# An adaLN transformer block on one core: four VectorE operations and one GpSimd group put elsewhere in the hand-written order

## The reference

```python
h = layernorm(x) * (1 + ca) + sa
Q, K, V = h @ Wq.T + bq, h @ Wk.T + bk, h @ Wv.T + bv      # 16 heads of 16
Q, K = elu(Q) + 1, elu(K) + 1
KV = einsum('bshd,bshe->bhde', K, V);  K_sum = K.sum(axis=1)
Z = 1 / (einsum('bshd,bhd->bsh', Q, K_sum) + 1e-6)
x = x + ga * (einsum('bshd,bhde,bsh->bshe', Q, KV, Z) @ Wo.T + bo)
h = layernorm(x) * (1 + cb) + sb
logits = cosine(h, centroids) + h @ w_route.T              # 8 experts
gates = softmax over the two largest logits, else 0
x = x + gb * sum_e gates_e * (gelu(h @ w1_e + b1_e) @ w2_e + b2_e)
```

## Time and profile before

| what | value |
|---|---|
| median of 3 runs | 365.79 us (365.43 to 366.67) |
| profiled execution, its own time | 366.65 us |
| its span | 364.6 us |
| TensorE busy | 349.9 us (96%) |
| VectorE, GpSimd, ScalarE busy | 286.7, 260.5, 234.0 us |
| granted TensorE clock | 1.00 |

### The profile page before, as it was taken

One profiled execution on the slowest core, in us unless ns is written; L12 is line 12 of the kernel. 1 busy time (PEld: TensorE's weight loads), 2 busy tenths in 40 slices (PEclk: granted clock), 3 DMA queues, 4 the chain that ended last, 5 costly groups with the idle time before them and its releaser, 6 DMA issues.

```text
span 364.6 us, 8796 instructions
## 1 busy us (share of the span) xinstructions
PE 349.9 (96%) x2780; PEld 327.3 (90%) x2780; DVE 286.7 (79%) x820; ACT 234.0 (64%) x516; POOL 260.5 (71%) x358
## 2 busy tenths in 40 slices
PE   7999999998999996899999999999999999999995
PEld 7877888887888996899998999999999999999895
DVE  4769767567776989989999898898898988886754
ACT  4376787888978764648557485584674855855541
POOL 4346899877977667787897878889889877655210
PEclk9999999999999999999999999999999999999999
DMA  7941640000000032142240322422314314324211
GB/s 267 331 155 34 202 144 0 2 1 2 0 2 3 1 119 89 40 135 89 61 144 21 127 90 60 135 79 78 104 54 131 87 58 145 89 59 146 93 54 58
DMA packets 23713, 31.79 MB, mean 87 GB/s; under 512 B 2288, under 2 KB 14204, under 8 KB 23680
## 3 DMA queue, kind: packets, MB, share of 16 engines
q1 hardware_dynamic: 23240, 31.34, 27.6%
q10 hardware_dynamic: 440, 0.04, 0.1%
HBM read 27.04 MB, written 4.34 MB: 86 GB/s over the span
## 4 chain that ended last, share of the span: by engine, by line
PE 75%; DVE 16%; issue 4%; DMA 2%; ACT 2%; DVEq 0%; ACTq 0%
PE bank L795 21%; PE bank L796 19%; PE bank L797 19%; PE bank L803 4%; PE bank L850 3%; DVE hid_g L1348 2%; PE bank L827 2%; DMA g_bc<-in_b 2%; DVE bank L1365 2%; PE bank L978 2%; DVE early L1265 1%; PE bank L903 1%; DVE gT_f L1404 1%; PE bank L1020 1%; DVE den L1296 1%
## 5 line engine op out<-in xcount | busy, mean ns | idle before, releaser
L738 ACT ACTIVATE bank<-bank,cols_sb 128x256 f32<-128x256 f32 x128 | 51.3, 438 | 43.1 <-PE bank L797 42.8
L795 PE MATMUL bank<-tr_hi,w_hi 128*128 128x256 f32 x256 | 73.4, 287 | 0.0
L796 PE MATMUL bank<-tr_lo,w_hi 128*128 128x256 f32 x256 | 72.3, 282 | 0.0
L797 PE MATMUL bank<-tr_hi,w_lo 128*128 128x256 f32 x256 | 72.1, 282 | 0.0
L795 PE MATMUL bank<-w_hi,hid_pair 128*128 128x256 f32 x252 | 70.6, 280 | 0.0
L797 PE MATMUL bank<-w_hi,hid_pair 128*128 128x256 f32 x252 | 70.4, 279 | 0.0
L796 PE MATMUL bank<-w_lo,hid_pair 128*128 128x256 f32 x252 | 70.4, 279 | 0.0
L501 POOL TENSOR_TENSOR hid_pair<-hid_g,hid_pair 128x512 fp32r<-128x512 f32 x42 | 54.3, 1294 | 7.0 <-POOL gT_r L526 3.3
L795 PEld LDWEIGHTS bank<-tr_hi,w_hi 128*128 128x128 f32 x256 | 48.8, 191 | 0.3 <-DVE hid_g L1348 0.2
L797 PEld LDWEIGHTS bank<-tr_hi,w_lo 128*128 128x128 f32 x256 | 48.9, 191 | 0.0
L796 PEld LDWEIGHTS bank<-tr_lo,w_hi 128*128 128x128 f32 x256 | 48.8, 191 | 0.0
(11 more groups left out here) (161 smaller groups left out, 934.0 us busy)
## 6 DMA issues: line engine op xcount, KB each, us to landing
g_bc<-g_dram SPq DMA_DIRECT2D x64, 256.0 KB, 3.5
x_sb<-in_x SPq DMA_DIRECT2D x16, 256.0 KB, 3.7
out<-x_sb SPq DMA_DIRECT2D x15, 256.0 KB, 2.3
early<-in_wmod SPq DMA_DIRECT2D x3, 512.0 KB, 7.4
q_sb<-in_w SPq DMA_DIRECT2D x2, 512.0 KB, 6.4
q_sb<-in_w SPq DMA_DIRECT2D x1, 1024.0 KB, 10.3
mod_row<-mod_dram SPq DMA_DIRECT2D x1, 1024.0 KB, 6.6
q_sb<-in_wqkvT SPq DMA_DIRECT2D x2, 384.0 KB, 5.7
```

The costliest lines, as they stand in the source:

```text
L738: last = ac.activation(half, half, ACT.Gelu, bias=b1_sb[:, e:e + 1])
L795: te.matmul(out_ap, l_hi, r_hi, start=start, stop=False, skip_group_check=shared)
L796: te.matmul(out_ap, l_hi, r_lo, start=False, stop=False, skip_group_check=shared)
L797: return te.matmul(out_ap, l_lo, r_hi, start=False, stop=stop, skip_group_check=shared)
```

## The change

Three places. On VectorE, in projection steps 9 and 10 (UPB is 8), stats_a(u+3) runs ahead of the key-sum copy and the masks, no longer at the end of the step. On VectorE, in expert steps 0 to 4, lo_o(u+3) runs ahead of denominators(u+4) and, in steps 1 to 4, of gate(u,0); in step 0 keep_ksum(1) runs behind lo_o(3). On GpSimd, rstd_e(2) moves from the end of step -1 into step 0, behind lo_e(0,0) and exp_gates(1). Nothing is added or left out.

```diff
@@ GpSimd, step_e
                 if u.plus(1):
                     exp_gates(u.plus(1))
                 if u.nth(0):
+                    rstd_e(unit(2))
                     lo_e(u, 1)
...
-                if u.plus(3):
+                if u.plus(3) and not u.nth(-1):
                     rstd_e(u.plus(3))
@@ VectorE, step_e
+            def first_steps(u):
+                return any(u.nth(j) for j in range(5))
...
                 if u.nth(0):
                     gate(u, 0)
                     gate(u, 1)
-                    keep_ksum(1, bank[6][:, 0:E])
                 if u.plus(1):
                     gates_a(u.plus(1))
...
                 if u.nth(5):
                     lo_m(1, bank[7])
+                if first_steps(u):
+                    lo_o(u.plus(3))
+                if u.nth(0):
+                    keep_ksum(1, bank[6][:, 0:E])
                 if u.plus(4) and not u.nth(-1):
                     denominators(u.plus(4))
                 if u and not u.nth(0):
                     gate(u, 0)
-                if u.plus(3):
+                if u.plus(3) and not first_steps(u):
                     lo_o(u.plus(3))
@@ VectorE, step_a
+                if u.plus(3) and (u.nth(UPB + 1) or u.nth(UPB + 2)):
+                    stats_a(u.plus(3))
                 if u.nth(UPB + 1):
                     keep_ksum(0, bank[0][:, 0:E])
                     ve.memset(kv_m[:, :, :], 0.0)
                     mask_kv(0, 0)
...
-                if u.plus(3):
+                if u.plus(3) and not u.nth(UPB + 1) and not u.nth(UPB + 2):
                     stats_a(u.plus(3))
```

## The result

The changed kernel takes 367.95 us (median of 22 executions, 365.96 to 369.78), the kernel before 365.89 us (22, 365.11 to 366.67): a ratio of 1.0051 with a 95% interval of 1.0038 to 1.0064. The forecast was no change that can be measured, 365.9 us with a range to 367.1; the change costs about 2 us.

What follows compares the result with a forecast made beforehand. TensorE was taken as the bound, so only shorter TensorE stalls count. The terms -0.14 + 0 + 0 + 0.24 = +0.1 us gave 365.9 us from a median of 365.79, no measurable difference, range 364.4 to 367.1.

Steps and rivals of the forecast that it cites:

- part 2: Expert step 0: attend(3) starts 1.34 us earlier, but TensorE idles later instead, likewise in step 1; worth 0.
- Part 1: Projection steps 9 and 10, statistics ahead of the masks: make_prod(0) starts earlier, place_kv ends earlier; -0.14 us.
- The port: Rival, chance 0.06: GpSimd's power holds the second half of place_kv through the shared port; +0.5 us, total 366.5.
- the masks held twice: Rival, chance 0.17: half masks wait for make_prod(0), then the powers of rstd_a(13); make_m(0) +1.1 us, total 367.1.
- The powers in step 0: GpSimd's rstd_e(2) behind exp_gates(1): normalise_e(2) ends at 139.9, modulate_e(2) needs it at 140.2; cost 0, margin 0.3 us.
- Part 3: Expert steps 1 to 4, lo_o early: VectorE waits for ScalarE's copy, the stall before attend(7) goes; +0.24 us.
- the sign: New TensorE stalls of 0.5 us before second(2,0) and second(3,0), named as showing the forecast right.
- Early copy: Rival, chance 0.30: VectorE doesn't stand in steps 2 and 3, attend(7)'s stall falls without a price; -0.88 - 0.14, total 364.8.
- signs named for a right forecast: attend(3), attend(4) over 1.2 us earlier, tp_e(2), second(1,0) not; VectorE idle 0.7; new stalls 0.5; attend(7) none; make_m(0) within 0.3.

Runs made afterwards that it cites:

- step 0 alone: Kernel before with lo_o(3) early in expert step 0 only, rstd_e(2) and keep_ksum(1) in their new places: 366.42 us, ratio 1.0012 [0.9998, 1.0026].
- step 1 alone: Kernel before with only lo_o(4) moved early in expert step 1: 367.62 us, ratio to the kernel before 1.0032 [1.0011, 1.0054].
- step 4 alone: Kernel before with only lo_o(7) moved early in expert step 4: 365.77 us against 366.27, ratio 0.9976 [0.9957, 0.9996].
- attend(4) doubled: Changed kernel with the products of attend(4) in expert step 1 computed twice: 366.57 us, ratio to the kernel before 1.0008 [0.9989, 1.0026].

## Why the prediction was wrong

**The step that failed** is the value of part 2: "So the 1.40 us of step 0, and the like one of step 1, are worth **0**". The reasoning before it held. attend(3) came early (136.28, forecast 136.95, of which 0.75 is the shift of the whole timeline), tp_e(2) and second(1,0) stayed tied to VectorE, and TensorE "idles later instead". But idle time was priced by its sum alone. Two pieces of 1.40 and 0.83 us became one of 2.09, and 1.10 and 0.33 became one of 1.75 (1.20 where TensorE comes there late) just ahead of another 0.57, and behind these the granted clock fell to half for 3.4 us. The sum has no clock term, and "The granted clock is 1.00 in both" was taken as a fact of the kernel where it was a result of its order. Measured: 0.4 to 0.7 us for the stretch of step 0, mostly there (in 10 of 12 executions of step 0 alone), and 1.5 to 1.6 us for that of step 1 (in 9 of 12 of step 1 alone). By their clocks 21 of 34 timed executions of the changed kernel had both (15 of 22 and 6 of 12). With the forecast's 365.9 that makes 366.3 to 366.6 for the one and 367.8 to 368.2 for both; the groups have their medians at 366.4 and 368.3.

- **Part 1** (-0.14): right in size, 0 within the error (0.9991 [0.9977, 1.0006]), with -0.06 on the stall in the trace. It went as forecast: the statistics lasted 1.01 us, the masks got 1.17 us shorter, and place_kv ended 2.32 us behind the start of make_prod(0) (87.73 - 85.41), as in the earlier trace rows.
- **The port and the masks held twice** did not happen. place_kv runs 0.61 us while GpSimd's power starts in the middle of it, at 87.39, just as in the earlier trace rows; its second half starts 0.03 us behind the power and takes 0.30 us. By the rule that I cited (the Trainium skill, SBUF — State Buffer, "SBUF: two separate sides") it could have been held; the trace doesn't bear that out for this pair, as far as 0.03 us tell which came first. For w_lo beside split_lo it does: 1.38 us instead of 0.36 before, beside a GpSimd operation of 1.31 us. Nobody was waiting for w_lo.
- **The powers in step 0** held up nothing, with less to spare than forecast: normalise_e(2) ended at 139.33 and modulate_e(2) started at 139.42, 0.09 us in place of 0.3.
- **Part 3** (+0.24): VectorE stood 0.64 us in step 2 (0.72 forecast), second(2,0) and second(3,0) stalled 0.33 us each (the sign named 0.5), attend(7) not at all. Counted from second(1,0), TensorE was 0.67, 0.94 and 0.15 us later than before at second(2,0), second(3,0) and second(4,0); forecast were 0.67, 1.0 and 0.24. Mechanism and sizes right, and the whole under what can be measured (0.9999 [0.9981, 1.0016] with only these steps).
- **Early copy** did not come true in step 2, since VectorE waits there. Where the copy is in time, in step 4 alone, a gain was seen: 0.9976 [0.9957, 0.9996].
- **The range** missed by 0.85 us, since it was made of rivals in which only waits change. All signs named for a right forecast that concern waits came true, but for the size of the two new stalls; none of them looked at the clock.

Not settled: why a given execution falls behind such a piece of idle and another doesn't. Step 1 alone did both in its two profiles, and step 0 alone both by its means. Nor was it tried from how much crowded idle on it begins (0.33 and 0.57 in step 1 of the kernel before never did it, 1.20 and 0.57 did once), or how far the work on either side counts. The prices of the second stretch come from one pair of profiles each, those of the first from four profiles.

## What to carry to other kernels

Where TensorE is the bound, price idle time by how it is spread and not by its sum alone: taking one of two short stalls away, when the next wait ends at the same time as ever, joins them and can, as here, cost a stretch at half clock. Such a change can be recognised beforehand (an early start whose next wait is pinned by another engine) and tested cheaply by filling the gap with repeated products; if the kernel gets faster with more work, idle time is the cause. Keep such a move only where the stall stands alone, as in step 4.

## What the runs showed of the hardware that I had not expected

- The granted clock falls to the lower level behind 1.8 to 2.3 us of idle, in one piece or two close ones, in a kernel whose TensorE is busy 96% of the span, and comes back 3.4 us later (six stretches in five profiles, worked out from the clocks of windows of 2 us). Behind 1.40 and 0.83 us, with three microseconds of work between them, it doesn't fall in the profile of the kernel before, and by mean clock and span in none of its 87 executions beside the experiments.
- With the same instructions in the same order it falls in some executions and not in others, so the median of a kernel with such a place is that of a mixture, and one profile may show none of it: of the five timed runs with such a gap (the change twice, attend(4) doubled, step 0 alone, step 1 alone), two have a profile with a clock of 1.00 throughout steps 0 and 1.
- The price depends on what follows, at the same length of 3.4 us: 0.4 to 0.7 us where TensorE soon waits for VectorE anyway, 1.5 to 1.6 us where TensorE runs without stalls.
